# Second layer: values with ones as the weights, probabilities moving, two heads in the array's column halves

## What is computed

```python
xn = layer_norm(x, norm_w, norm_b)
q = (xn @ q_w + q_b).reshape(Bx, Tx, H, -1)
k = (xn @ k_w + k_b).reshape(Bx, Tx, H, -1)
att = jnp.einsum('bnhl,bmhl->bnmh', q, k)
mask = src_mask.reshape(Bx, 1, Tx, 1)
att = att + (1.0 - mask) * -1000000.0
att = jax.nn.softmax(att, axis=2)
v = ((xn @ v_w + v_b) * src_mask[:, :, None]).reshape(Bx, Tx, H, -1)
y = jnp.einsum('bnmh,bmhl->bnhl', att, v).reshape(Bx, Tx, Dx)
e = jax.nn.silu(emb) @ emb_w + emb_b
scale, shift = jnp.split(e[:, None, :], 2, axis=2)
h = layer_norm(y, sb_norm_w, sb_norm_b) * (1.0 + scale) + shift
h = jax.nn.silu(h) @ out_w + out_b
return x + h
```

## Time and profile before

| | us |
|---|---|
| median of 3 runs (2406.51 to 2408.11) | 2408.03 |
| profiled execution | 2409.56 |
| its span, first to last instruction | 2407.8 |
| TensorE matmuls busy | 2338.5 |
| TensorE weight loads busy | 2087.5 |
| VectorE busy | 1483.3 |
| ScalarE busy | 823.3 |
| GpSimd busy | 575.4 |

### The profile page before, as it was taken

One profiled execution on the slowest core, in us unless ns is written; L12 is line 12 of the kernel. 1 busy time (PEld: TensorE's weight loads), 2 busy tenths in 40 slices (PEclk: granted clock), 3 DMA queues, 4 the chain that ended last, 5 costly groups with the idle time before them and its releaser, 6 DMA issues.

```text
span 2407.8 us, 43859 instructions
## 1 busy us (share of the span) xinstructions
PE 2338.5 (97%) x15670; PEld 2087.5 (87%) x15670; DVE 1483.3 (62%) x3441; ACT 823.3 (34%) x1893; POOL 575.4 (24%) x847
## 2 busy tenths in 40 slices
PE   8999999999999999986999999999999999999998
PEld 5888888888888888865999999999999998989897
DVE  4677777777777777745555555555555555555644
ACT  2233333333333333331333333333333333333332
POOL 0332222233333333312121212121212121212120
PEclk9999999999999999987999999999999999999997
DMA  6210100000101000002535353535353434444441
GB/s 236 83 35 31 35 35 35 35 35 35 35 35 35 35 35 31 31 36 62 124 88 123 88 123 88 123 90 122 93 118 97 114 101 111 104 107 108 103 104 48
DMA packets 90933, 187.14 MB, mean 78 GB/s; under 512 B 18708, under 2 KB 29394, under 8 KB 90904
## 3 DMA queue, kind: packets, MB, share of 16 engines
q1 hardware_dynamic: 88856, 186.23, 29.2%
q10 hardware_dynamic: 2048, 0.53, 0.1%
HBM read 51.81 MB, written 33.69 MB: 36 GB/s over the span
## 4 chain that ended last, share of the span: by engine, by line
PE 47%; ACT 4%; DVE 3%; issue 1%; SPq 0%; DMA 0%; DVEq 0%; POOL 0%; POOLq 0%
PE bank L1430 7%; PE bank L439 6%; PE bank L441 6%; PE bank L440 6%; PE bank L1420 5%; PE bank L431 4%; PE bank L432 4%; PE bank L430 4%; PE bank L1446 3%; ACT g L1304 2%; PE bank L1379 1%; PE bank L1369 1%; DVE top L1163 1%; DVE hs L1204 1%; ACT th L1310 1%
## 5 line engine op out<-in xcount | busy, mean ns | idle before, releaser
L439 PE MATMUL bank<-xT_hi,w_hi 128*128 128x256 f32 x1536 | 445.7, 290 | 2.6 <-DVE xT_lo L1146 1.4
L440 PE MATMUL bank<-xT_lo,w_hi 128*128 128x256 f32 x1536 | 447.3, 291 | 0.0
L441 PE MATMUL bank<-xT_hi,w_lo 128*128 128x256 f32 x1536 | 444.6, 289 | 0.0
L1155 DVE SCALAR_TENSOR_TENSOR parts<-bank,qk_bias,parts 128x256 fp32r<-128x256 f32 x256 | 112.1, 479 | 431.3 <-ACT parts L1287 431.3
L1430 PEld LDWEIGHTS bank<-v,prob 128*128 128x128 f32 x2048 | 317.6, 195 | 12.7
L430 PE MATMUL bank<-w_hi,xT_hi 128*128 128x512 f32 x768 | 322.5, 420 | 0.0
L432 PE MATMUL bank<-w_lo,xT_hi 128*128 128x512 f32 x768 | 322.2, 419 | 0.0
L431 PE MATMUL bank<-w_hi,xT_lo 128*128 128x512 f32 x768 | 319.6, 416 | 0.0
L439 PEld LDWEIGHTS bank<-xT_hi,w_hi 128*128 128x128 f32 x1536 | 292.3, 190 | 4.7 <-DVE xT_lo L1146 1.8
L440 PEld LDWEIGHTS bank<-xT_lo,w_hi 128*128 128x128 f32 x1536 | 292.5, 190 | 1.8
L1430 PE MATMUL bank<-v,prob 128*128 128x33 f32 x2048 | 293.3, 251 | 0.0
(11 more groups left out here) (163 smaller groups left out, 4167.4 us busy)
## 6 DMA issues: line engine op xcount, KB each, us to landing
stack<-parts SPq DMA_DIRECT2D x768, 128.0 KB
xr<-in_x SPq DMA_DIRECT2D x32, 512.0 KB, 3.5
x_between_layers<-x SPq DMA_DIRECT2D x64, 256.0 KB, 2.0
xr<-x_between_layers SPq DMA_DIRECT2D x32, 512.0 KB, 3.6
out<-y_out SPq DMA_DIRECT2D x64, 256.0 KB, 2.0
w_emb<-in_L_cond_W_emb SPq DMA_DIRECT2D x4, 1024.0 KB, 9.7
w_emb<-in_L_cond_emb_w SPq DMA_DIRECT2D x4, 1024.0 KB, 4.9
raw<-in_L_cond_Wq SPq DMA_DIRECT2D x1, 1024.0 KB, 5.8
```

Of the source, the lines that this page charges most:

```text
L439: yield nc.tensor.matmul(dst, w_hi[:, m, c, fs], a_hi[:, c], start=(first and c == 0), stop=False)
L440: yield nc.tensor.matmul(dst, w_hi[:, m, c, fs], a_lo[:, c], start=False, stop=False)
L441: yield nc.tensor.matmul(dst, w_lo[:, m, c, fs], a_hi[:, c], start=False, stop=(c == C - 1))
L1155: nc.vector.scalar_tensor_tensor(parts[:, LO[n], c].rearrange("p b t -> p (b t)"), ps[QK_BANKS[n][c // 2]][:, at:at + PAIR * P], qk_bias[: ...
```

## The change

`mixed` swaps the operands: `v` of a head, now 64 columns wide (32 values and 32 of ones), is the weight operand, and `prob`, 128 columns, moves. Even heads use the left half of the array's columns and write partitions 0 to 63 of the bank, odd heads the right half and partitions 64 to 127 (`tile_position`). The result is transposed: 32 rows of outputs and 32 equal rows of sums for each head, queries along the columns. ScalarE copies it into the part of `prob` that is no longer needed (`copy_yT`), and TensorE transposes it back, two heads at a time (`turned`), into the same banks. From there VectorE goes on as before, with heads 64 columns apart instead of 33.

The order changes with it. `mixed` runs as two blocks behind query projections 0 and 1 instead of woven; `turned` is woven with query projections 2 and 3 and with the values. VectorE takes the last two low parts of the queries after the outputs of batch 0 and the norm of the next pair, instead of before. Four of the 24 stack copies, those of the queries' low parts, are issued by ScalarE after its last high part and a wait for the low parts, instead of by SyncE. Of the scores of batch 0, eight products instead of four run ahead of the weave.

The diff, without the names of the semaphores `yT_ps` and `yT`, the wait of `values`, which is for `yT_ps` now, and the two calls of `copy_yT` in ScalarE's tail:

```diff
     BV, BO = 1, 2
-    DV = DH + 1
+    DV = 2 * DH
     HB = 512 // P
...
             rows(0, Q_HI, 2)
-            sp.wait_ge(s["qk_lo"], seq(2 * C, i, 2 * C))
-            rows(0, Q_LO, 1)
 
...
 
-        def qk_low(i, n):
-            for c in range(C):
+        def qk_low(i, n, chunks):
+            for c in chunks:
                 if c % 2 == 0:
...
         def body(i, first, more, last):
-            qk_low(i, 1)
+            qk_low(i, 1, range(C))
             if not last:
                 row_stats(i + 1, (i + 1) % RING)
-            qk_low(i, 0)
+            qk_low(i, 0, (0, 1))
             if not first:
                 end_outputs(i - 1, 0)
             if not last:
                 norm(i + 1, (i + 1) % RING)
+            qk_low(i, 0, (2, 3))
             if not first:
...
 
+        def query_low_rows(i):
+            act.wait_ge(s["qk_lo"], seq(2 * C, i, 2 * C))
+            for a in range(HC):
+                act.dma_start(f32(stack[DH:2 * DH, 0, a]),
+                              f32(parts[DH * a:DH * a + DH, Q_LO])).then_inc(s["stack"], 16)
+
         def exps(prev, b):
             for j in range(C):
                 act.wait_ge(s["w_ps"], seq(PAIR * C, prev, b * C + j + 1))
                 nc.scalar.activation(prob[:, b, HB * j:HB * j + HB, :],
                                      ps[W_BANKS[j]][:, :].rearrange("p (h t) -> p h t", h=HB),
                                      ACT.Exp).then_inc(s["prob"], 1)
+
+        def copy_yT(prev, b):
+            for k in range(2):
+                act.wait_ge(s["yT_ps"], seq(2 * PAIR, prev, 2 * b + k + 1))
+                nc.scalar.activation(prob[:, b, C * k:C * k + C, :].rearrange("p h t -> p (h t)"),
+                                     ps[Y_BANKS[b][k]][:, :], ACT.Copy).then_inc(s["yT"], 1)
 
...
                 exps(i - 1, 1)
-            qk_high(i, 0, range(C))
+                copy_yT(i - 1, 0)
+            qk_high(i, 0, (0, 1))
+            if not first:
+                copy_yT(i - 1, 1)
+            qk_high(i, 0, (2, 3))
+            query_low_rows(i)
             if not first:
...
 
-
             pe.wait_ge(s["prob"], seq(PAIR * C, prev, C + 2 * (b + 1)))
             for h in range(H):
-                j, a = h // HY, h % HY
-                last = nc.tensor.matmul(ps[Y_BANKS[b][j]][:, a * DV:(a + 1) * DV], prob[:, b, h, :], v[:, b, h, :],
-                                        start=True, stop=True)
+                q, half = h // 2, slice(DV * (h % 2), DV * (h % 2) + DV)
+                last = nc.tensor.matmul(ps[Y_BANKS[b][q // C]][half, (q % C) * P:(q % C + 1) * P], v[:, b, h, :],
+                                        prob[:, b, h, :], start=True, stop=True, tile_position=(0, DV * (h % 2)))
+                if h % HY == HY - 1:
+                    last.then_inc(s["yT_ps"], 1)
+
+        def turned(prev, b):
+
+            pe.wait_ge(s["yT"], seq(2 * PAIR, prev, 2 * (b + 1)))
+            for q in range(HY):
+                last = nc.tensor.transpose(ps[Y_BANKS[b][q // C]][:, (q % C) * P:(q % C + 1) * P], prob[:, b, q, :],
+                                           ident[:])
+                if q == HY - 1:
+                    last.then_inc(s["y_ps"], 1)
                 yield
-            last.then_inc(s["y_ps"], 1)
 
...
                     weight_scores(i - 1, f // 2)
-            run(projected(i, 0, (0, 1)))
-            if first:
-                run(projected(i, 0, (2, 3)))
-            else:
-                woven(several(2, projected(i, 0, (2, 3))), mixed(i - 1, 0))
-            outputs1, values0 = () if first else mixed(i - 1, 1), value_rows(i, 0)
-            woven(outputs1, values0, Z_AFTER)
+            run(projected(i, 0, (0,)))
+            if not first:
+                mixed(i - 1, 0)
+            run(projected(i, 0, (1,)))
+            if not first:
+                mixed(i - 1, 1)
+            woven(projected(i, 0, (2, 3)), () if first else turned(i - 1, 0))
+            woven(value_rows(i, 0), () if first else turned(i - 1, 1))
             if not first:
                 z_transposed(i - 1, 0)
-            run(outputs1)
-            run(values0)
             values1 = value_rows(i, 1)
...
                 z_transposed(i - 1, 1)
-            run(islice(scores0, 2))
+            run(islice(scores0, 4))
             woven(outputs0, scores0)
...
         for b in range(PAIR):
-            run(mixed(NP - 1, b))
+            mixed(NP - 1, b)
+        for b in range(PAIR):
+            run(turned(NP - 1, b))
         for b in range(PAIR):
```

More of the change, by code:

```diff
@@ L1003, in layer1 @@
         "qk_ps", "qk_hi", "qk_lo", "stack", "v_ps", "v", "s_ps", "top", "top_ps", "top_T",
-        "shift0", "shift1", "w_ps", "prob", "y_ps", "p_sum", "y", "y_stats", "y_var", "y_var_eps", "y_rstd", "z",
+        "shift0", "shift1", "w_ps", "prob", "yT_ps", "yT", "y_ps", "p_sum", "y", "y_stats", "y_var", "y_var_eps", "y_rstd", "z",
         "z_ps", "gains", "g", "tanh", "silu", "h_hi", "h_lo", "o_ps", "out", "stored")}
@@ L1190, in values @@
             if not first:
-                dve.wait_ge(s["y_ps"], seq(PAIR, i - 1, b + 1))
+                dve.wait_ge(s["yT_ps"], seq(2 * PAIR, i - 1, 2 * (b + 1)))
             nc.vector.scalar_tensor_tensor(v[:, b, :, 0:DH], ps[V_BANKS[b]][:, :].rearrange("p (h d) -> p h d", h=H),
@@ L1353, in _ @@
         exps(NP - 1, 1)
+        copy_yT(NP - 1, 0)
+        copy_yT(NP - 1, 1)
         for b in range(PAIR):
```

## The result

The changed kernel takes 2432.26 us, median of 4 runs (2430.2 to 2434.27); the kernel before took 2407.27 in the same comparison (4 runs). The ratio is 1.0105, 95% interval 1.0087 to 1.0122: slower by 25 us, where 16 us faster was forecast. The profiled execution took 2433.04 us, its span is 2431.2, against 2407.8.

The account below looks back on a forecast made before the run. TensorE was taken as the bound, its matmuls filling 97% of the span. A body of 9.45 + 20.35 + 9.3 = 39.1 us saves 0.66, times 31 bodies: 2408 - 20 + 3 = 2391 us, range 2362 to 2490.

Parts of the forecast that it names:

- M: Mixing time of one second-layer body: 4.2 us, between 3.6 and 8.1, with neighbouring heads overlapping in the array's halves.
- changes between whole and half arrays: Cost in the mixing of switching the array four times a body: up to 1.0 us, taken as 0.6.
- rival of products one after another: Mixing halves do not overlap: M 7.1 to 8.1, time 2480 up to 2511; partly or wholly so, chance 0.42.
- B: Body part with queries, mixing, values and transposes, up to the first score: 20.35 us, ended by the stack; 20.29 before.
- High part: ScalarE's high part of the last queries, in B: done 0.85 us after the bank is full, at 5.7 + M + 0.9.
- A: First part of a second-layer body, keys and weight scores: 9.45 us, kept unchanged in the sum.
- one gap ahead of the scores: TensorE's first gap before the scores at the end of B, released by the stack: near 1 us.
- the 1.2 that it took between the stack and TensorE's own work: End of B: stack ready at 16.15 + M, 1.2 us later than TensorE's own 14.9 + M.
- C: Last body part, scores woven with the output projection: 9.3 us instead of 10.02, the stop for a maximum going.
- fall to 1.2 GHz: Sign that would show the forecast wrong: TensorE dropping its clock at the new wait; no size or chance given.
- tail: After the last body, without cover: two copies and eight transposes at half clock, about 3 us.
- general formula: Change in kernel time over 31 bodies plus the tail, for any mixing time: 31 x (M - 4.86) + 3.

Follow-up runs that it names:

- the instruction moved on VectorE: Changed kernel with VectorE's end_norm of batch 1 moved ahead of end_silu of batch 0, so z is ready earlier: 2447.46 us.
- The filler: Changed kernel plus seven TensorE products a body that nobody reads, covering both pauses: 2397.84 us, ratio to before 0.9958.
- neighbours in the same half: Changed kernel with heads in another order, four even then four odd, so most neighbours share a half of the array's columns: 2460.62 us.
- late mixing with silu first: The late mixing kernel with VectorE's silu of batch 0 ahead of end_norm of batch 1 and values of batch 0 behind it: 2361.35 us.
- late mixing: Changed kernel with batch 1's mixing behind the queries, four value products ahead of its transposes back, and VectorE normalising earlier: 2367.13 us.
- before, with five more copies: Kernel before with five extra copies into unread stack rows behind the last stack copies, TensorE's program unchanged: 2559.62 us.

## Why the prediction was wrong

**The mixing, M.** Predicted 4.2 us a body. A block of 32 records takes (1.97 - 0.27) / 31 = 0.055 a record. From the last projection's start at 1715.45, a projection's 0.12 later would be 1715.57; the next one starts at 1717.56, and the one after it 0.10 later than its pitch: 1.99 + 0.10 = 2.09 a block, 4.2 a body. For one block 32 x 0.055 = 1.76 is streaming and 0.33 the two changes between whole and half arrays, 0.65 a body where I took 0.6. The Trainium skill's page "TensorEngine Tiling (Array Packing)" has both, the factor of up to two (Theoretical Speedup) and the drain (Key Properties); the trace agrees with the first (0.055 us a record where 0.109 is the pitch in one half), and if all that is lost at the changes is the drain, a change and the change back cost 0.33 us. The rival of products one after another is out.

**B.** Predicted 20.35, measured 20.77. It ends with the stack, as said. High part: 11.65 predicted, 11.9 measured. TensorE is through the queries 10.84 us after A (1724.93 less 1714.09; 10.8 predicted), but the last product's result is there 0.2 later, which is when ScalarE starts, and the sum had no term for that:

```profile
1724.93 0.40 PE L430 MATMUL bank<-w_hi,xT_hi 128*128 128x512 f32 x1
1725.13 0.84 ACT L1286 ACTIVATE parts<-bank,qk_bias 128x256 fp32r<-128x256 f32 x2 [3.34 <-PE bank L441]
```

From there to the first score 8.7 predicted, 8.9 measured. Each term was within 0.25 us, but they add to 0.4 x 31 = 13 us, which is most of the gain. The prediction looked for one gap ahead of the scores, near 1 us and released by the stack. There are two: the 0.80 for z of batch 1, which it had nowhere, and 0.51 for the stack. Together they are near the 1.2 that it took between the stack and TensorE's own work, and the first costs nothing by itself, since without it B is as long (20.8 us with the instruction moved on VectorE).

**C.** Predicted 9.3; measured 10.02 - (12.98 - 12.34) = 9.38. Right: the wait for the maximum went, because gate and tanh run during the pause. But this saving hangs on the pause: with the order that has none, C is 10.04 again.

**The clock: the step that failed.** The sum says "what TensorE saves in mixing it waits at the scores", and prices that wait at nothing beyond its length. I named the fall to 1.2 GHz only as what would make the prediction wrong, with the reason that the body shows no such stop now, which is why it could not be taken for harmless: the longest pause of a body before is 0.11 us (in C, where the prediction's half microsecond counts what starts come late by), the new ones are 0.80 and 0.51. They brought 1.2 GHz in 10 of 28 bodies at 3.1 us each, 31 us. With it and the 13 of B the sum is 2391 + 13 + 31 = 2435, where 2432 was measured; the 3 us for the tail are not seen (from the end of the 28 bodies to the last instruction 115.1 us before, 114.8 now). The filler shows it directly: with the pauses covered and all else equal the kernel is at 2397.8, which is 9 us faster than before, on the side forecast and inside the forecast's own range of 2362 to 2403.

**The rivals.** None had it. The measured time lies in the span between the forecast and the case of one after another, but by another mechanism. A rival "TensorE pauses, and the clock falls" could have been named from the profile before, where the lower clock is seen at the second layer's start and end, at about double pitch for as long as it lasts (a transpose 0.27 instead of 0.11); how often and how long it would fall no row could tell.

**Slips in the working.** Two, and nothing rests on them: TensorE's B before is 20.3 by the terms given, not 20.1 (20.29 measured), and M = 4.6 gives 2403 by the general formula, not 2404.

**What stays open.** Why with the same two pauses a body falls in one case and the next does not, and how often for a pause of a given length, is not settled here. The runs show only that it happens more often with longer pauses, and not smoothly: with neighbours in the same half the pauses are as long as in the changed kernel and 6 bodies fall instead of 10, and the 29th body of the changed kernel, with pauses of 0.77 and 1.14 us, did not fall.

## What to carry to other kernels

Where TensorE is never idle, a change that moves the end of a stage to another engine or a DMA can have two prices, the wait and the clock behind it. In this kernel pauses of 1.3 to 1.8 us in a body cost 1.6 or 3.1 us more in 6 to 24 of 28 bodies, and one of 1.95 us cost 3.1 in all of them: give such a pause a price and a chance of its own. Shorten first the chain that would end last (here: put the mixing behind the projections that feed the copies), then take the saving. A pause that can't be removed can be covered with products that nobody reads, and removing one wait can be a loss if it merges two pauses into a longer one. What another chain gains while the engine pauses (C here) is gone with the pause.

## What the runs showed of the hardware

The pauses of TensorE in a body (medians of the 28), and what followed:

| kernel | pauses, us | bodies of 28 with a stretch at 1.2 GHz |
|---|---|---|
| before | 0.10 | 0 |
| late mixing with silu first | 0.10 | 0 |
| late mixing | 0.22 | 0 |
| changed, both pauses covered | none noted | 0 |
| changed, first pause covered | 0.54 | 0 |
| changed, neighbours in the same half | 0.80 and 0.51 | 6 |
| changed | 0.80 and 0.54 | 10 |
| changed, z earlier | 1.54 | 22 |
| changed, low rows by SyncE | 0.42 and 1.34 | 24 |
| before, with five more copies | 1.95 | 28 |

A stretch cost 3.1 us, in the kernel before with its pause as in the changed one, or 1.6 in a shorter form: 41.1 or 41.5 us against 39.5 or 39.95 in the two kernels with pauses of 1.54 and 1.34, and once 42.3 against 40.7 with neighbours in the same half.

Two half-array fp32 products ran as fast as one: single records of 128 moving columns start in pairs 0.007 us apart, a pair every 0.109 us, which is what one record takes where only one half has work. The weight loads of 64 columns, 0.137 us a piece, add nothing to that:

```profile
L1447 PEld LDWEIGHTS bank<-prob,v x2048: 132/137/231, 1146.7 to 2406.3; 128*64 128x64 f32 x187
```
